# Cross attention of a fused attention and expert kernel rebuilt: heads on halves of TensorE, late normalisation, a ring of eight x tiles, and paced transfers

## The chip, the cores and the metric

The kernel runs on one core of a Trainium2 chip. The metric is the device time of one execution in microseconds (us), median of three runs. One core has five engines that are programmed apart and meet at semaphores: TensorE (PE; matmuls and transposes into PSUM, which has 8 banks of 128 x 512 floats), VectorE (DVE), ScalarE (ACT), GpSimd (POOL, which doesn't read PSUM here) and SyncE (SP, which only issues DMAs here). Each engine runs its own list of instructions strictly in order.

## The reference, cut to what matters

```python
def xattn(q, k, v, gamma):               # q: (4, 512, 512); k = v = ctx, same shape; 8 heads
    qh, kh, vh = (a.reshape(B, 8, 64, 512) for a in (q, k, v))
    qk = einsum('bhdq,bhdl->bhql', qh, kh) / sqrt(64)
    return gamma * einsum('bhql,bhdl->bhdq', softmax(qk, -1), vh).reshape(B, 512, 512)
x = x + xattn(layernorm(x), ctx_2048, ctx_2048, gamma)
h = layernorm(x).reshape(-1, 512)        # 2048 rows
# shared expert, 1408 wide, times a sigmoid gate; router: softmax over 8, top 2, weights normed
# routed experts, 352 wide: silu(h @ w_gate[e]) * (h @ w_up[e]) @ w_down[e], weighted by the router
x = x + routed + sigmoid(h @ shared_gate_w) * shared
```

Everything is float32. A matmul operand a is split into a rounded high part (type fp32r) and the rest, and a product is made of three terms, hi*hi, hi*lo and lo*hi, each an fp32r matmul. A row of 64 consecutive rows of x is one head's query, so a tile of 128 rows is two heads.

## The kernel before, in words

**Stages.** Attention over 16 tiles (NT) of 128 rows; then the shared expert in 4 blocks of 512 rows by 11 chunks of 128 hidden columns (`gate_up`, `down`, `weights_hi`, `weights_lo`); then 39 slots of 128 rows for the routed experts. All three are written out as one list for each engine.

**One attention tile.** SP loads x (`xb`), the context tile twice over (`cn` in rows, `cd` with each head's 64 rows doubled onto 128 partitions) and x a second time (`x2b`). DVE takes the row moments, POOL the inverse deviation and the shift (`rstd`, `nmr`), ACT writes the normed rows (`xn`, L657) and the high part of the queries (`qs`, L668), POOL their low part (L531). POOL splits the doubled keys (`kh`, `kl`). A head's `qs` has high and low part on the two halves of the partitions, against the doubled keys, so that two matmuls (L1233, L1234) give all terms of a score block of 128 x 512: 16 matmuls a tile. DVE takes the row maximum (L924), ACT the exponential with the row sum (L681), DVE the reciprocal, and POOL multiplies the probabilities by it (L548). Only then does PE transpose them (`probs_T`, L1241, 4 transposes for each of 8 groups), ACT and DVE split them (`pth` L687, `ptl` L933), and three matmuls for each group (L1254, L1255, L1257) sum the output of both heads in one bank. DVE adds gamma times that to `x2b` (L939). One tile later the new rows are normed (ACT, L661), transposed (`rows_T`), evicted (`x2T`, L693) and used for the router (`logits`), and stored three times: `x_rows`, `x_normed_rows`, `x_normed_transposed`.

**Order.** Every engine's list is written by hand in `tile(t, ...)`: tiles 0 to 3 and the last two are written out, the ten between run as a loop on each engine (`over_tiles`, `Fori`). PE works on head 0 and 1 of tile t while the scores of tile t + 1 are slipped in between.

**Start.** SP issues the loads of tiles 0 and 1, a few small ones, two zero tiles and then `slot_rows` (L378), a table of 4992 entries of 8 bytes, and behind it the loads of tile 2.

**End of attention.** PE ends tile 15, runs the first chunk of the shared expert (`gate_up(0, 0)`), then `rows_T(15)` and `logits(15)`, then the second chunk. SP stores the last `x2T` (L362) and only then issues the loads of weight chunk 2 (`load_chunk`, L389). ACT waits for the stores, then runs silu of chunk 0, `weights_hi(2)`, which waits for chunk 2, and `hidden_hi(0)`, on which `down(0, 0)` (L1361) waits through DVE.

## Time and profile before

| | |
|---|---|
| median of 3 runs (lowest, highest) | 927.79 us (927.32, 928.38) |
| the profiled execution: its own time | 931.45 us |
| its span, from first to last instruction | 929.1 us |
| mean granted TensorE clock | 0.985 of full speed |
| PE busy | 871.1 us, 94% of the span |
| attention, to the first matmul of the shared expert | 0 to 283.7 us |
| shared expert | 283.7 to about 646 us |
| routed experts | about 646 to 929 us |

The page of the profile gives busy times by engine and the chain of work that ended last. A matmul's record lasts until its result is complete (0.39 us for 512 columns), and the next starts before that, so the distance between starts is the price of one in a stream. A line of the timeline merges instructions that follow each other with the same shape and source line: start, time covered, engine, line, operation, what is written and read, count, and in brackets the idle time before it and what ended it.

### The profile page before, as it was taken

What the parts mean: (1) busy time and instruction counts of PE and PEld (TensorE: products, weight loads), DVE (VectorE), ACT (ScalarE), POOL (GpSimd) and SP (SyncE); (2) the same over time, 40 slices, a digit from 0 to 9 for tenths busy, and PEclk for the clock granted to TensorE, in tenths of its full rate; (3) what the DMA queues carried; (4) which work ended last, traced back from release to release, by engine and by line L of the source; (5) the groups of instructions that cost most, each with busy time, mean ns of one, the idle gap of its engine ahead of it and who ended that gap; (6) DMA issues with size and microseconds to landing.
All of it is one profiled execution on the core that took longest, in us unless ns stands there. A gap on an engine that the chain in (4) does not pass through costs nothing.

```text
span 929.1 us, 14497 instructions
## 1 busy us (share of the span) xinstructions
PE 871.1 (94%) x4560; PEld 746.0 (80%) x4560; DVE 571.9 (62%) x920; ACT 519.0 (56%) x879; POOL 477.9 (51%) x460
## 2 busy tenths in 40 slices
PE   4798998999998999999999999999999999999993
PEld 3587777877776888888888888888899999999992
DVE  5587878787874653442121212113899999999892
ACT  5588788887884432112111111112688888888881
POOL 5587787878740000004333000000589999999984
PEclk9899999999999999999999999999999999999997
DMA  9435334253553431400032002553954344443542
GB/s 135 86 101 158 116 123 149 97 162 103 161 190 127 134 102 46 136 0 1 1 137 25 0 1 91 187 187 104 335 104 86 74 83 75 79 80 68 91 62 40
DMA packets 70142, 93.77 MB, mean 101 GB/s; under 512 B 16137, under 2 KB 35593, under 8 KB 70098
## 3 DMA queue, kind: packets, MB, share of 16 engines
q1 hardware_dynamic: 60338, 72.73, 26.7%
q0 software_dynamic: 9760, 20.49, 12.4%
q8 instruction: 24, 0.39, 0.2%
q14 instruction: 20, 0.16, 0.1%
HBM read 65.59 MB, written 27.60 MB: 100 GB/s over the span
## 4 chain that ended last, share of the span: by engine, by line
PE 70%; ACT 2%; DVE 1%; issue 1%; DMA 0%; POOL 0%; POOLq 0%; SPq 0%; ACTq 0%; DVEq 0%
PE bank L1347 8%; PE bank L1349 8%; PE bank L1348 8%; PE bank L1414 5%; PE bank L1416 5%; PE bank L1415 5%; PE bank L1361 4%; PE bank L1363 4%; PE bank L1362 4%; PE bank L1439 3%; PE bank L1438 3%; PE bank L1440 3%; PE bank L1371 2%; PE bank L1425 1%; PE bank L1241 1%
## 5 line engine op out<-in xcount | busy, mean ns | idle before, releaser
L1035 DVE TENSOR_TENSOR sg<-bank,sg 128x512 f32<-128x512 f32 x44 | 30.4, 692 | 208.8 <-PE bank L1349 200.0
L1347 PE MATMUL bank<-x_hl,wsp 128*128 128x512 f32 x352 | 137.1, 390 | 0.0
L1349 PE MATMUL bank<-x_hl,wsp 128*128 128x512 f32 x352 | 137.0, 389 | 0.0
L1348 PE MATMUL bank<-x_hl,wsp 128*128 128x512 f32 x352 | 137.0, 389 | 0.0
L593 POOL DMA_INDIRECT slot_rows<-msrc,posi x32 | 36.1, 1128 | 176.2 <-PE bank L1349 169.8
L608 POOL DMA_INDIRECT xg<-x_normed_rows,meta x39 | 39.8, 1021 | 159.7 <-PE bank L1371 142.1
L787 ACT ACTIVATE sg<-bank 128x512 f32<-128x512 f32 x44 | 26.3, 598 | 158.4 <-PE bank L1349 158.4
L687 ACT ACTIVATE pth<-bank 128x512 fp32r<-128x512 f32 x128 | 73.4, 598 | 52.0 <-PE bank L1241 50.4
L933 DVE TENSOR_TENSOR ptl<-bank,pth 128x512 fp32r<-128x512 f32 x128 | 85.9, 682 | 21.1 <-ACT pth L687 20.9
L548 POOL TENSOR_SCALAR pb<-pb,rinv 128x512 f32<-128x512 f32 x128 | 87.7, 699 | 13.2 <-DVE rinv L929 7.8
L794 ACT ACTIVATE hh<-sg 128x512 fp32r<-128x512 f32 x44 | 27.8, 631 | 114.2 <-DVE sg L1035 99.5
L681 ACT ACTIVATE pb<-bank,negmax 128x512 f32<-128x512 f32 x128 | 86.9, 689 | 0.7 <-DVE negmax L924 0.3
L924 DVE TENSOR_REDUCE negmax<-bank 128x1 f32<-128x512 f32 x128 | 81.9, 681 | 0.7 <-PE bank L1234 0.2
L629 POOL TENSOR_TENSOR wd<-wex,wd 96x512 fp32r<-96x512 f32 x39 | 76.3, 1957 | 3.3
L1233 PE MATMUL bank<-kh,qs 128*128 128x512 f32 x128 | 57.9, 453 | 21.2 <-POOL qs L531 18.1
L1241 PE MATMUL bank<-ident,pb 128*128 128x128 f32 x512 | 72.9, 276 | 4.6 <-POOL pb L548 4.6
L619 POOL DMA_INDIRECT out<-y,meta x39 | 71.0, 1821 | 11.9 <-issue 5.7
L1349 PEld LDWEIGHTS bank<-x_hl,wsp 128*128 128x128 f32 x352 | 66.1, 188 | 13.7
L1348 PEld LDWEIGHTS bank<-x_hl,wsp 128*128 128x128 f32 x352 | 66.1, 188 | 13.7
L1347 PEld LDWEIGHTS bank<-x_hl,wsp 128*128 128x128 f32 x352 | 66.1, 188 | 13.7
L1241 PEld LDWEIGHTS bank<-ident,pb 128*128 128x128 f32 x512 | 62.3, 143 | 15.9 <-POOL pb L548 5.5
L1361 PE MATMUL bank<-wsp,hh 128*128 128x512 f32 x176 | 68.8, 391 | 2.3 <-DVE hl L1037 1.7
(157 smaller groups left out, 2354.2 us busy)
## 6 DMA issues: line engine op xcount, KB each, us to landing
cd<-in_ctx SPq DMA_DIRECT2D x32, 256.0 KB, 4.8
wex<-in_L_ffn_w_gate SPq DMA_DIRECT2D x8, 704.0 KB, 4.3
...
```

Source lines behind the costliest of these rows:

```text
L548: gp.tensor_scalar(pb[s][:, q, :], pb[s][:, q, :], rinv[:, s, q:q + 1], 0.0, ALU.mult, ALU.add).then_inc(g_pn, 1)
L619: g.indirect_dma_start(out=out, out_offset=bass.IndirectOffsetOnAxis(ap=meta[:, s, 0:1], axis=0), in_=y3[s % 2][:, :], in_offset=None, com ...
L629: gp.tensor_tensor(wd3[0:IR, 1, c], wex[0:IR, e, 2 * W3 + (IC - 1) * H:EW], wd3[0:IR, 0, c].bitcast(F32), ALU.subtract).then_inc(g_wd, 1)
L681: sc.activation(pb[s][:, q, :], bS[q][:, :], ACT.Exp, bias=negmax[:, s, q:q + 1], scale=1.0, accum_out=rsum[:, s, q:q + 1]).then_inc(a_exp, 1)
L687: sc.activation(pth[c][:, :], bT[c % 2][:, :], ACT.Copy).then_inc(a_pth, 1)
L924: ve.tensor_reduce(negmax[:, s, q:q + 1], bS[q][:, :], AX_X, ALU.max, negate=True).then_inc(d_max, 1)
L933: ve.tensor_tensor(ptl[c][:, :], bT[c % 2][:, :], pth[c][:, :].bitcast(F32), ALU.subtract).then_inc(d_ptl, 1)
L1241: ins = te.transpose(bT[c % 2][:, q * P:(q + 1) * P], pb[s][:, q, c * P:(c + 1) * P], ident[:, :])
L1347: te.matmul(bk[:, :], hi, xhi, start=(h == 0), stop=False)
L1348: te.matmul(bk[:, :], hi, xlo, start=False, stop=False)
L1349: ins = te.matmul(bk[:, :], lo, xhi, start=False, stop=(h == HC - 1))
L1361: te.matmul(bY[tt][:, :], th, hi, start=(c == 0), stop=False)
```

## The change

Nothing changes from the shared expert on, but for three points at the seam. In attention:

- **Scores.** Each head's queries and keys stay on their own 64 partitions (`qh`, `ql`, `kh`, `kl`, 128 x 512 each). For one block of 128 query columns, `scores(t, c)` runs three terms for both heads: six matmuls over 64 partitions, alternately partitions 0 to 63 into one PSUM bank and 64 to 127 into the next. 24 matmuls of 64 partitions a tile stand for 16 of 128. The context is loaded once, not three times.
- **Maxima** go over both heads at once (128 x 1024, four a tile in place of eight of 128 x 512).
- **Normalisation** moves behind the value product. PE transposes the unnormed probabilities as soon as the exponentials are done. POOL spreads the eight reciprocals over 64 columns each (`spread`), PE transposes that (`inverses`, 4 transposes more), ACT evicts it times gamma (`rgam`), and POOL multiplies the attention output by it (`scaled`) and adds x (`residual`).
- **Values.** A head's high and low values stand side by side as one 128-column weight, so two matmuls a group do in place of three; the two halves of the result are added by an ACT copy (`low_half`) and a DVE addition over 64 partitions (`halves`), for each head.
- **Engines.** The normed rows and the high parts of the queries move from ACT to POOL.
- **Ring and pace.** x is loaded once into a ring of 8 buffers, in which the new rows are made in place. SP lets each load off at a count of PE's transposes (`paced`).
- **Loop.** All engines' steps are written out (`over_tiles` from -4 to 18), but for PE, whose steps 4 to 13 are a loop over pairs.
- **Seam.** `gate_up(0, 0)` comes after step 16, then step 17 (`rows_T(14)`, `logits(14)`), `gate_up(0, 1)`, and step 18 (`rows_T(15)`, `logits(15)`). Block 0 and chunks 0 and 1 are loaded in step 12.

In a middle tile, on SP: the stores of the new rows and the loads of the context. Before (`xb`, `cd` and `cn` are loads; `x2b` both):

```order
L356 DMA x_rows<-x2b_96 128x512 [waits d_x2]
L358 DMA x_normed_rows<-x2n_98 128x512 [waits a_x2n]
L352 DMA x2b_96<-in_x 128x512 [waits st_x21,a_x2n]
L344 DMA cn_71<-in_ctx 128x512 [waits e_vt]
L335 DMA xb_70<-in_x 128x512 [waits a_xn]
L340 DMA cd_74<-in_ctx 64x2x512 [waits kl_done]
L340 DMA cd_74<-in_ctx 64x2x512
```

Now (`g_x2` counts `residual` on POOL):

```order
L352 DMA x_rows<-xb_84 128x512 [waits g_x2]
L356 DMA x_normed_rows<-x2n_109 128x512 [waits g_x2n]
L343 DMA cn_69<-in_ctx 128x512 [waits kl_done,e_vt,e_t]
L360 DMA x_normed_transposed<-x2T_111 128x512 [waits a_x2T]
L338 DMA xb_81<-in_x 128x512 [waits st_x20,g_x2n,e_t]
```

Before, the store waited for DVE's L939, and keys came in `cd`; now the load of `cn`, keys and values of step i + 2, stands behind the store of the rows of tile i - 1.

On POOL in the same place. Before:

```order
L538 TENSOR_SCALAR kh_75<-cd_73 128x1024 [waits ld_cd0,e_s]
L548 TENSOR_SCALAR pb_86<-pb_86,rinv 128x512 [waits d_rinv]
L548 TENSOR_SCALAR pb_86<-pb_86,rinv 128x512
L519 TENSOR_TENSOR rstd<-vare,mhalf 128x1 [waits d_vare1,a_x2n]
L521 TENSOR_SCALAR nmr<-aggr,rstd 128x1 [waits g_rstd1]
L531 TENSOR_TENSOR qs_82<-xn_80,qs_82 64x512 [waits a_qh,g_nmr1]
```

Now (`d_att` counts `halves`; L562 is `scaled`, L566 `residual`):

```order
L562 TENSOR_TENSOR att_104<-att_104,rgam 128x512 [waits a_Rg,d_att]
L516 TENSOR_SCALAR nmr<-aggr,rstd 128x1 [waits g_rstd1]
L566 TENSOR_TENSOR xb_85<-xb_85,att_104 128x512 [waits g_att]
L522 TENSOR_SCALAR xn<-xb_88,rstd,nmr 128x512 [waits g_nmr0]
L539 CAST kh_72<-cn_70 128x512 [waits e_s,ld_cn1]
L528 CAST qh_76<-xn 128x512 [waits e_s,g_xn]
L550 TENSOR_SCALAR x2n_109<-xb_84,rstd,nmr 128x512 [waits e_x2T,st_x2n1,g_nmr1]
L533 TENSOR_TENSOR ql_78<-xn,qh_76 128x512 [waits g_qh]
L543 TENSOR_TENSOR kl_74<-cn_70,kh_72 128x512 [waits g_kh]
```

The keys' high part used to be made a tile ahead of its use, between multiplications of probabilities; now the split of keys and queries follows `residual` directly, and `cn`'s landing is waited for inside it.

On PE at the seam. Before, behind the last matmul of `gate_up(0, 0)`:

```order
L1275 MATMUL bank<-ident,x2n_98 128x128 [waits a_lg,a_x2n]
L1275 MATMUL bank<-ident,x2n_98 128x128 x3
L1281 MATMUL bank<-rgT,x2T_100 128x9 [waits a_x2T]
L1281 MATMUL bank<-rgT,x2T_100 128x9 x3
L1347 MATMUL bank<-x_hl,wsp_104 128x512 [waits d_wl]
```

Now, behind the last matmul of `gate_up(0, 1)`:

```order
L1259 MATMUL bank<-ident,x2n_109 128x128 [waits g_x2n,a_x2T]
L1259 MATMUL bank<-ident,x2n_109 128x128 x3
L1265 MATMUL bank<-rgT,x2T_111 128x9 [waits a_x2T,a_lg]
L1265 MATMUL bank<-rgT,x2T_111 128x9 x3
L1362 MATMUL bank<-wsp_113,hh_130 128x512 [waits d_hl,g_x2,a_lg]
```

Tile 15's transposes moved behind 24 more matmuls, and `down(0, 0)` follows them directly. The diff, cut to its core:

```diff
         big = cursor[0]
...
-        vs = [place(f"vs{j}", [P, 2, LC, 3, DH], F32R) for j in range(2)]
-        pb = [place(f"pb{j}", [P, QC, L]) for j in range(2)]
+        kh = [place(f"kh{j}", [P, L], F32R) for j in range(2)]
+        kl = [place(f"kl{j}", [P, L], F32R) for j in range(2)]
+        qh = [place(f"qh{j}", [P, L], F32R) for j in range(2)]
...
+            def load_x(t):
+                after(sp, g_x2n, t - NX + 1)
+                after(sp, st_x2[t % 2], 16 * ((t - NX) // 2 + 1))
+                sp.dma_start(xb[t % NX][:, :], x_t[t, :, :]).then_inc(ld_x[t % NX], 16)
...
+            def load_values(t):
+                after(sp, e_vt, t - 1)
                 after(sp, kl_done, t - 1)
-                for half in range(2):
-                    sp.dma_start(cd[par][DH * half:DH * (half + 1), :, :], c_h[t, :, :, :]).then_inc(ld_cd[par], 16)
-            def load_values(t, par):
-                after(sp, e_vt, t - 1)
-                sp.dma_start(cn[par][:, :], c_t[t, :, :]).then_inc(ld_cn[par], 16)
...
+            def paced(t, n):
+                if there(t):
+                    sp.wait_ge(e_t, 8 * t + n)
+            def store_rows(t):
+                sp.wait_ge(g_x2, t + 1)
+                sp.dma_start(x2_t[t, :, :], xb[t % NX][:, :]).then_inc(st_x2[t % 2], 16)
...
+            def step(i):
+                if there(i - 1):
+                    store_rows(i - 1)
+                if there(i - 3):
+                    store_normed(i - 3)
+                if there(i + 2):
+                    paced(i - 1, 8)
+                    load_values(i + 2)
+                if there(i - 3):
+                    store_columns(i - 3)
+                if there(i + 4):
+                    paced(i, 3)
+                    load_x(i + 4)
...
+            load_x(0)
+            load_values(0)
+            load_x(1)
+            load_values(1)
+            load_x(2)
+            small_ones()
+            load_x(3)
+            for i in range(NT + 3):
+                step(i)
...
-            def power(kind, n):
-                after(g, (a_xn, a_x2n)[kind], n)
-                g.wait_ge(d_vare[kind], n + 1)
-                gp.tensor_tensor(rstd[:, kind, :], vare[:, kind, :], mhalf[:, :], ALU.pow).then_inc(g_rstd[kind], 1)
-                wait_ahead(g, g_rstd[kind], n + 1)
-                gp.tensor_scalar(nmr[:, kind, :], aggr[:, kind, 0:1], rstd[:, kind, :], -1.0, ALU.mult, ALU.mult).then_inc(g_nmr[kind], 1)
...
-            def queries_lo(t, s, par, before, count):
-                g.wait_ge(before, count)
-                g.wait_ge(a_qh, 2 * t + s + 1)
-                r = slice(DH * s, DH * (s + 1))
-                o = slice(DH * (1 - s), DH * (2 - s))
-                gp.tensor_tensor(qs[s][o, :], xn[par][r, :], qs[s][r, :].bitcast(F32), ALU.subtract).then_inc(ql_done, 1)
...
+            def queries(t):
+                g.wait_ge(g_nmr[0], t + 1)
+                gp.tensor_scalar(xn[:, :], xb[t % NX][:, :], rstd[:, 0, t % 2, :], nmr[:, 0, t % 2, :], ALU.mult, ALU.add).then_inc(g_xn, 1)
...
+                g.wait_ge(g_xn, t + 1)
+                after(g, e_s, 8 * t - 8)
+                gp.tensor_copy(qh[t % 2][:, :], xn[:, :]).then_inc(g_qh, 1)
...
-            def norm_p(k, s, pair):
-                wait_ahead(g, d_rinv, 2 * k + pair + 1)
-                for q in (2 * pair, 2 * pair + 1):
-                    gp.tensor_scalar(pb[s][:, q, :], pb[s][:, q, :], rinv[:, s, q:q + 1], 0.0,
-                                     ALU.mult, ALU.add).then_inc(g_pn, 1)
...
+            def step(i):
+                if there(i + 1):
+                    queries(i + 1)
+                    keys_hi(i + 1)
+                    queries_hi(i + 1)
+                if there(i - 3):
+                    rows_normed(i - 3)
+                if there(i + 1):
+                    queries_lo(i + 1)
+                    keys_lo(i + 1)
+                if there(i - 2):
+                    inverse_deviation(1, i - 2)
+                if there(i + 2):
+                    inverse_deviation(0, i + 2)
+                if there(i):
+                    spread(i)
+                if there(i + 2):
+                    shift(0, i + 2)
+                if there(i - 1):
+                    scaled(i - 1)
+                if there(i - 2):
+                    shift(1, i - 2)
+                if there(i - 1):
+                    residual(i - 1)
...
+            def inverses(t):
+                act.wait_ge(e_R, t + 1)
+                after(act, g_att, t)
+                sc.activation(rgam[:, :], bT[1][:, :], ACT.Copy, scale=gam[:, :]).then_inc(a_Rg, 1)
+            def low_half(t, s):
+                act.wait_ge(e_pv, 8 * t + 4 * s + 4)
+                after(act, d_att, 2 * t - 1 + s)
+                lo, hi = slice(DH * (1 - s), DH * (2 - s)), slice(DH * s, DH * (s + 1))
+                sc.activation(lob[hi, :], bO[lo, :], ACT.Copy).then_inc(a_lob, 1)
...
-            def maxima(k, s, pair):
-                after(dve, a_exp, 4 * k - 4)
-                for q in (2 * pair, 2 * pair + 1):
-                    dve.wait_ge(e_s, 4 * k + q + 1)
-                    ve.tensor_reduce(negmax[:, s, q:q + 1], bS[q][:, :], AX_X, ALU.max, negate=True).then_inc(d_max, 1)
...
+            def maxima(t, c):
+                dve.wait_ge(e_s, 8 * t + 2 * c + 2)
+                after(dve, a_exp, 8 * t + 2 * c - 6)
+                ve.tensor_reduce(negmax[:, c, :], bSS[c % 2][:, :, :], AX_X, ALU.max, negate=True).then_inc(d_max, 1)
...
+            def halves(t, s):
+                dve.wait_ge(a_lob, 2 * t + s + 1)
+                after(dve, g_x2, t - 1)
+                r = slice(DH * s, DH * (s + 1))
+                ve.tensor_tensor(att[t % 2][r, :], bO[r, :], lob[r, :], ALU.add).then_inc(d_att, 1)
...
+            def scores(t, par, c):
+                if c == 0:
+                    pe.wait_ge(ql_done, t + 1)
                     pe.wait_ge(kl_done, t + 1)
-                after(pe, a_exp, 4 * k - 4 + 2 * pair + 2)
-                for q in (2 * pair, 2 * pair + 1):
-                    te.matmul(bS[q][:, :], qs[s][:, q * P:(q + 1) * P], kh[par][:, s, :], start=True, stop=False)
-                    te.matmul(bS[q][:, :], qs[s][:, q * P:(q + 1) * P], kl[par][:, s, :], start=False, stop=True).then_inc(e_s, 1)
...
+                after(pe, a_exp, 8 * t + 2 * c - 2)
+                terms = ((qh, kh), (qh, kl), (ql, kh))
+                for n, (a, b) in enumerate(terms):
+                    for s in range(2):
+                        r = slice(DH * s, DH * (s + 1))
+                        ins = te.matmul(bSS[c % 2][:, s, :], a[par][r, c * P:(c + 1) * P], b[par][r, :], start=(n == 0), stop=(n == 2))
+                        if n == 2:
+                            ins.then_inc(e_s, 1)
...
-                    ins = te.transpose(bT[c % 2][:, q * P:(q + 1) * P], pb[s][:, q, c * P:(c + 1) * P], ident[:, :])
+                    ins = te.transpose(bT[P_BANK[n]][:, q * P:(q + 1) * P], pb[par][s][:, q, c * P:(c + 1) * P], ident[:, :])
...
-                hi, lo = (vs[par][:, a, c, s:s + 2, :].rearrange("p a d -> p (a d)") for a in range(2))
-                first, last = s == 0 and c == 0, s == 1 and c == LC - 1
-                pe.wait_ge(a_pth, 4 * k + c + 1)
-                te.matmul(bO[:, :], hi, pth[c][:, :], start=first, stop=False)
-                te.matmul(bO[:, :], lo, pth[c][:, :], start=False, stop=False)
-                pe.wait_ge(d_ptl, 4 * k + c + 1)
-                te.matmul(bO[:, :], hi, ptl[c][:, :], start=False, stop=last).then_inc(e_pv, 1)
+                if c == 0:
+                    after(pe, d_att, 2 * t + s)
+                v = vs[par][:, c, 2 * s:2 * s + 2, :].rearrange("p a d -> p (a d)")
+                pe.wait_ge(a_pth, 8 * t + n + 1)
+                te.matmul(bO[:, :], v, pth[n % 4][:, :], start=(c == 0), stop=False)
+                pe.wait_ge(d_ptl, 8 * t + n + 1)
+                te.matmul(bO[:, :], v, ptl[n % 4][:, :], start=False, stop=(c == LC - 1)).then_inc(e_pv, 1)
...
+                pe.wait_ge(g_rspr, t + 1)
+                for c in range(QC):
+                    ins = te.transpose(bT[1][:, c * P:(c + 1) * P], rspr[:, 2 * c:2 * c + 2, :].rearrange("p s d -> p (s d)"), ident[:, :])
+                ins.then_inc(e_R, 1)
...
-                    values_T(t + 1, i + par, 1 - par)
...
+                        gate_up(b, c, par)
                     if b == 0 and c == 1:
                         pe.wait_ge(a_lg, NT)
-                        pe.wait_ge(d_x2, NT)
+                        pe.wait_ge(g_x2, NT)
...
                 if last:
                     rows3(1, 0, 1)
-            logits(NT - 2, 0)
+            for i in range(-4, 4):
+                step(i, i // 2, i % 2)
+            with pe.Fori(2, NI - 1) as half:
+                for par in range(2):
+                    step(2 * half + par, half, par)
+            for i in range(NT - 2, NT + 1):
+                step(i, i // 2, i % 2)
             gate_up(0, 0, 0)
-            rows_T(NT - 1, 1)
-            logits(NT - 1, 1)
+            step(NT + 1, (NT + 1) // 2, (NT + 1) % 2)
+            gate_up(0, 1, 0)
+            for i in range(NT + 2, NT + 3):
+                step(i, i // 2, i % 2)
             for b in range(NB):
                 block2(b, b % 2, b == NB - 1)
```

## Rows read from the trace of the kernel before

**Rows 1.** The page: the span.
```profile
span 929.1 us, 14497 instructions
```
**Rows 2.** Windows: stretch, length, busy us (count) of each engine, clock, DMA share, GB/s.
```profile
180.00:220.00 40.00, 37.23 (x222) 31.27 (x221) 32.00 (x67) 32.92 (x76) 32.38 (x40) 1.00 0.41 125
```
**Rows 3.** Timeline: PE's value transposes (L1265) seven tiles apart, the next group behind one.
```profile
151.38 0.60 PE L1265 MATMUL bank<-ident,cn 128*128 128x128 f32 x4
...
151.81 0.60 PE L1241 MATMUL bank<-ident,pb 128*128 128x128 f32 x4
...
263.54 0.60 PE L1265 MATMUL bank<-ident,cn 128*128 128x128 f32 x4
```
**Rows 4.** Waits of PE from 30 to 260 us: us in total, times, longest.
```profile
PE bank L1233 <- POOL qs L531: 18.1, 18, 1.5
```
**Rows 5.** Groups by line, 100 to 220 us: count | busy us, mean ns | idle before.
```profile
L548 POOL TENSOR_SCALAR pb<-pb,rinv 128x512 f32<-128x512 f32 x60 | 41.1, 700 | 3.4 <-POOL qs L531 3.4
L681 ACT ACTIVATE pb<-bank,negmax 128x512 f32<-128x512 f32 x60 | 40.7, 689 | 0.2
L933 DVE TENSOR_TENSOR ptl<-bank,pth 128x512 fp32r<-128x512 f32 x60 | 40.2, 681 | 7.5 <-ACT pth L687 7.5
L924 DVE TENSOR_REDUCE negmax<-bank 128x1 f32<-128x512 f32 x59 | 37.8, 681 | 0.3
L687 ACT ACTIVATE pth<-bank 128x512 fp32r<-128x512 f32 x60 | 34.4, 598 | 20.4 <-PE bank L1241 19.5
...
L542 POOL TENSOR_TENSOR kl<-cd,kh 128x1024 fp32r<-128x1024 f32 x8 | 19.2, 2395 | 0.0
```
**Rows 6.** Timeline of the start: the one DVE instruction over 128 x 1024.
```profile
8.39 1.21 DVE L949 TENSOR_TENSOR kl<-cd,kh 128x1024 fp32r<-128x1024 f32 x1
```
**Rows 7.** Timeline of PE: matmuls of 9 partitions between matmuls of 128.
```profile
15.38 0.40 PE L1233 MATMUL bank<-kh,qs 128*128 128x512 f32 x1
15.62 0.39 PE L1234 MATMUL bank<-kl,qs 128*128 128x512 f32 x1
15.94 0.41 PE L1292 MATMUL bank<-ident,rg 9*128 9x9 f32 x4
16.28 0.50 PE L1233 MATMUL bank<-kh,qs 128*128 128x512 f32 x1
```
**Rows 8.** The start: timeline, the landing of `slot_rows`, windows around the stall.
```profile
8.23 0.49 SPq L378 DMA_DIRECT2D slot_rows<-meta  x1
...
20.19 1.09 PE L1241 MATMUL bank<-ident,pb 128*128 128x128 f32 x8 [2.71 <-POOL pb L548]
...
30.00 0.69 DVE L896 BATCH_NORM_STATS2 stats<-xb 128x6 f32<-128x512 f32 x1 [3.71 <-DMA xb<-in_x]
...
DMA to landing us min/median/max: 21.4/21.4/21.4
...
32.00:36.00 4.00, 2.17 (x9) 2.10 (x10) 1.16 (x3) 0.76 (x2) 3.74 (x6) 0.50 0.23 75
```
**Rows 9.** SP's issues in a middle tile, and `cn`'s landing, 100 to 240 us.
```profile
152.58 0.35 SPq L352 DMA_DIRECT2D x2b<-in_x  x1
153.03 0.40 SPq L344 DMA_DIRECT2D cn<-in_ctx  x1
...
DMA to landing us min/median/max: 2.7/2.9/3.3
```
**Rows 10.** Timeline of the end of attention.
```profile
268.31 1.03 PE L1241 MATMUL bank<-ident,pb 128*128 128x128 f32 x8
...
283.70 0.48 PE L1347 MATMUL bank<-x_hl,wsp 128*128 128x512 f32 x1
...
289.27 0.60 PE L1275 MATMUL bank<-ident,x2n 128*128 128x128 f32 x4
289.91 0.60 ACT L693 ACTIVATE x2T<-bank 128x512 f32<-128x512 f32 x1 [1.96 <-PE bank L1275]
...
298.86 0.47 PE L1361 MATMUL bank<-wsp,hh 128*128 128x512 f32 x1 [1.68 <-DVE hl L1037]
```

680 lines of the change are left out of this document (305 added, 375 removed).

## The prediction

> **What bounds the kernel now.** I read the windows first, then the groups by line, then the timelines of the start, a middle tile and the end of attention. Only attention changes. A middle tile lasts (263.54 - 151.38) / 7 = 16.02 us [rows 3]. In 40 us of it PE is busy 37.2, DVE 32.0, ACT 32.9, POOL 32.4 [rows 2], so per tile PE 14.9, DVE 12.8, ACT 13.2, POOL 13.0 us. PE bounds, and what it misses it waits mostly for POOL's low part of the queries, 18.1 us in 230 [rows 4]. Around that: the start, where PE's first transposes of probabilities stand at 20.19 and DVE waits for x until 30.00, behind a table of tiny packets that took 21.4 us from 8.23 [rows 8]; and the seam, where the first transposes of tile 15 stand at 268.31, the shared expert starts at 283.70 and its first `down` at 298.86 [rows 10]. I reckon to that `down`; what follows (929.1 - 298.9 = 630 us [rows 1, 10]) is unchanged.
>
> **The work per tile after.** PE: a group of four transposes costs 151.81 - 151.38 = 0.43 us [rows 3], a matmul of 512 columns 0.23 to 0.24 [rows 7]. One group more, +0.43; 8 value matmuls fewer, -1.84. The scores were 16 x 0.23 = 3.7. If the two heads' halves run side by side, 12 pairs cost 2.8 (-0.9); if they don't, 24 matmuls cost 5.5 (+1.8). The switch to smaller operands and back cost 0.32 and 0.34 us where a matmul follows after 0.24 [rows 7], so about 0.1 a switch and 8 x 0.1 = +0.8. PE: 14.9 + 0.43 - 1.84 - 0.9 + 0.8 = **13.4**, or **16.1** if the halves run in turn. No row has two matmuls on disjoint partitions, so the ends are 0.23 and 0.46 a pair. I take the low one: the two heads use other partitions and other PSUM banks, and the next weight is loaded beside a running matmul already.
> The Trainium skill (TensorEngine Tiling (Array Packing), Key Properties) says that tiles load and multiply in parallel, and that each change of the tiling mode drains the engine. The first would give 13.4 and the second speaks against the change; the 0.1 us of [rows 7] is all that this trace shows of such a drain.
> DVE: eight maxima of 0.68 [rows 5] become four of about 1.21, the one row over 1024 columns [rows 6]: -0.6; L939 goes, two `halves` come at 0.68: +0.6; six fewer tiny ones: -0.5. About **12.3**. ACT: four evictions and norms of queries and rows go (-2.9), three copies come at 0.60 (+1.8): **12.1**. POOL: eight multiplications of 0.70 go, the key split halves (L542 2.395 to 1.2 [rows 5]), five one-input passes at 0.70 and four two-input ones at 1.2 stay or come, plus 1.7 of tiny ones: **10**. On busy time alone a tile would be 13.4 plus the few tenths that PE loses to others, say 14.0. That the steps are written out, or loop on PE, I price at nothing: no row separates it, and PE would have 15.0 - 13.4 = 1.6 us a step to hide it (below); if that cover were gone I bound it at 0.3 us a step either way, 4 us in all.
>
> **The loop through the DMA.** The order makes a wait that busy time hides. SP's `store_rows(i-1)` waits for `residual(i-1)`, and the load of `cn` for tile i+2 is queued behind it. POOL needs that load for `keys_hi(i+2)`, nearly next in its list; behind it are queued the split of the queries, the normed rows of tile i-2 and `keys_lo`; PE's `scores(i+2, 0)` waits for these, and behind it stand the value products and the first transposes; DVE's maximum and, later, the next `halves`. From the end of `halves` of one step: `scaled` and `residual` 2 x 1.2 and 0.5 of handing over, 2.9; two store issues at 153.03 - 152.58 = 0.45 before the load [rows 9], 3.8; landing 2.9 [rows 9], 6.7; three passes at 0.70 and two at 1.2, 11.2; hand over, three pairs of scores, one value pair and a group of transposes with its end, 13.1; ACT's `pth` 0.60, 13.8; DVE's `ptl` 0.68, or PE's last value pair with ACT's `low_half`, 14.5; `halves` 0.68, 15.1 [rows 5]. So a step can't be shorter than about **15.0 us**, a us above what the engines need. With the landing at 2.7 or 3.3 [rows 9], and copies on POOL at 0.55 to 0.8 us, it is 14.5 to 15.5.
>
> **Start.** The first chain (moments, POOL's five passes, scores, maxima, exponentials) comes to the same 20.3 as before by my count: no wait for the norm on POOL, but four exponentials of each head must be done. The table now has 4 transfers of 256 KB fewer ahead of it and is issued some 2.5 us sooner; it should land near 26.5, not 29.6. x of tile 3 is behind it, and DVE's list has its moments first in step 1, from about 23: a wait of 3.4 us with all DVE work queued behind. Then a DVE step's work, 12.3 + 0.7: the first second-head `halves` ends at 39.4. Thirteen loops later: 39.4 + 13 x 15.0 = 234.4. Step 15 has no load to wait for; its first transposes stand some 9.9 us on, at **244.3** (before 268.3).
>
> **Seam.** From there to the shared expert before: 15.4 us [rows 10]. Now DVE has splits of tokens and two weight chunks in the same stretch, with one `halves` more: 15.9, at 260.2. Then `gate_up(0, 0)` 24 x 0.23 = 5.5; `rows_T(14)`, its eviction and `logits(14)` 2.2; `gate_up(0, 1)` 5.5; `rows_T(15)` to the end of its eviction 290.51 - 289.27 = 1.24 [rows 10]; from that end to `down(0, 0)` 298.86 - 290.51 = 8.35 [rows 10], a chain of store issue, load of chunk 2, `weights_hi(2)`, `hidden_hi(0)` and DVE that the change doesn't shorten. Sum 22.8: 283.0. Before, `gate_up(0, 1)` covered 5.5 of these 8.35 us; now nothing but `logits` is left, and PE stands for some 7.5 us. After the stall of the start the granted clock was 0.50, 1.2 in place of 2.4 GHz, for the 4 us of one window [rows 8]; 36 matmuls of 0.23 follow here, and half speed for 4 to 5 us costs +2.4: **285.4**. Before: 298.86.
>
> **Sum.** 298.9 - 285.4 = 13.4 us gained: span 915.7; the profiled execution would be 931.45 - 13.4 = 918.0, and the median, 3.7 below it before, **914.4 us**. Each 0.1 us a step is 1.3 us; the gain is gone at a step of 16.0.
>
> **Rivals.** (a) The loop doesn't bind, since the landing or POOL's passes are shorter, or the 7 us at the seam are covered: steps of 14.0, 914.4 - 13 = 901.4 us, or 904 by the seam alone. For it: POOL's 10 us of work. Against: the order leaves no way round. (b) More waits join the loop, since ACT and DVE must each be free just then and x2n's transposes wait for POOL too: a step of 15.9, 914.4 + 0.9 x 13 = 926 us. For it: three engines above 12 us and 15 us a step. (c) The two halves of the array run in turn. PE then has 16.1 us a tile, with 0.2 of waits 16.3: 914.4 + 1.3 x 13 = **931.3 us**, slower than before. It decides from 0.45 us a pair of score matmuls. Against: disjoint partitions and banks.
>
> **How the numbers follow.** Forecast 0.45, its own range 908 to 921; (a) 0.22, 893 to 908; (b) 0.20, 921 to 930; (c) 0.13, 926 to 938. Faster than by 0.2% (1.9 us, what this measurement can tell from no change) are the forecast, (a) and some 0.6 of (b): 0.79; within it 0.06; slower 0.15. Range 900 to 929.
>
> **What would show it.** Right: steps of about 15 us; POOL idle some 3 us a step before `kh` until DMA `cn` lands, 35 to 40 us in all; PE waiting for POOL `kl` at the first scores of a tile; `slot_rows` landing near 26; PE idle 7 us before the first `down`, clock 0.5 behind it. Score pairs 0.23 apart show the halves together, singles 0.23 apart show (c). No wait for `cn` with steps of 14 is (a). Wrong altogether: waits of ACT or DVE on instruction issue in the written-out steps.

## Result and the profile after

The changed kernel takes **930.5 us** (median of 20 runs, 926.3 to 935.3) beside 927.6 us for the kernel before on the same chips (20 runs, 921.7 to 933.0). The ratio is 1.0031 with an interval of 1.0016 to 1.0047: slower by 0.3%. The forecast was 914.4 us, with a range of 900 to 929. It was wrong by 16 us, and the sign was wrong.

The page of the changed kernel, its span and the busy time of each engine, beside [rows 1]:

```profile
span 927.5 us, 13748 instructions
## 1 busy us (share of the span) xinstructions
PE 859.2 (93%) x4624; PEld 713.7 (77%) x4624; DVE 573.2 (62%) x820; ACT 507.1 (55%) x863; POOL 433.5 (47%) x414
```

The span of the one profiled execution is 1.6 us *shorter* than before, while the medians say 2.9 us *longer*. So the two traces tell where time went, and the medians alone tell which kernel is faster. The profiled execution of before happened to lie 3.7 us above the median of its three runs; that of after lies 1.2 us below its own.

Windows of the changed kernel (stretch, length, busy us (count) of PE, PEld, DVE, ACT, POOL, granted clock, DMA share, GB/s): a stretch of attention, to be read against [rows 2], and the stretch of the seam.

```profile
180.00:220.00 40.00, 34.85 (x232) 25.40 (x230) 34.03 (x57) 32.26 (x77) 24.98 (x33) 1.00 0.39 128
...
260.00:300.00 40.00, 28.65 (x131) 23.35 (x132) 16.86 (x25) 16.50 (x25) 6.36 (x9) 0.83 0.43 139
```

PE had 37.2 of 40 us to do and now has 34.9, and no engine is full. The steps hardly shrank all the same. The value transposes (L1253) of tiles 2 and 15 stand at 37.54 and 242.51, so 13 steps take 15.77 us each, where [rows 3] gave 16.02 for seven middle ones and the same 13 took 16.16 before. Waits of the changed kernel from 40 to 250 us (engine, what it was to do, what it waited for: us in total, times, longest), beside [rows 4]:

```profile
POOL kh L539 <- DMA cn<-in_ctx: 43.5, 13, 4.4
...
PE bank L1259 <- POOL x2n L550: 15.5, 12, 2.3
POOL rspr L556 <- DVE rinv L922: 13.1, 13, 1.6
POOL att L562 <- DVE att L933: 12.6, 13, 1.2
```

POOL stands 3.3 us in each of 13 steps until `cn` has landed, and PE then waits for POOL. That is the loop which the prediction described. Its links in one middle step, from the timelines of DVE, POOL, SP and PE in turn (start, us, engine, line, operation; in brackets the idle time before it and its releaser):

```profile
144.17 0.69 DVE L933 TENSOR_TENSOR att<-bank,lob 64x512 f32<-64x512 f32 x1
...
159.63 0.69 DVE L933 TENSOR_TENSOR att<-bank,lob 64x512 f32<-64x512 f32 x1
```
```profile
144.95 1.28 POOL L562 TENSOR_TENSOR att<-att,rgam 128x512 f32<-128x512 f32 x1 [0.94 <-DVE att L933]
...
146.43 1.29 POOL L566 TENSOR_TENSOR xb<-xb,att 128x512 f32<-128x512 f32 x1
...
151.52 0.61 POOL L539 CAST kh<-cn 128x512 fp32r<-128x512 f32 x1 [3.04 <-DMA cn<-in_ctx]
...
154.65 1.28 POOL L543 TENSOR_TENSOR kl<-cn,kh 128x512 fp32r<-128x512 f32 x1
```
```profile
147.75 0.32 SPq L352 DMA_DIRECT2D x_rows<-xb  x1
148.11 0.43 SPq L356 DMA_DIRECT2D x_normed_rows<-x2n  x1
148.66 0.39 SPq L343 DMA_DIRECT2D cn<-in_ctx  x1
```
```profile
156.17 0.51 PE L1216 MATMUL scores<-kh,qh 64*128 64x512 f32 x2 [0.57 <-POOL kl L543]
...
157.64 0.60 PE L1225 MATMUL bank<-ident,pb 128*128 128x128 f32 x4
```

Read it as a ring. The second head's `halves` ends at 144.86; `scaled` and `residual` end at 147.72; SP had been held by the store of x_rows, issues it, then the store of the normed rows, then the load at 148.66; it lands 2.86 us later, at 151.52; the low part of the keys ends at 155.93; the scores follow, then transposes, ACT, DVE, and the next `halves` ends at 160.32. That is 2.86 + 0.94 + 2.86 + 4.41 + 4.39 = 15.46 us.

The seam, from the timeline of PE, beside [rows 10]: the first transposes of tile 15, the first `gate_up`, `rows_T(15)`, its `logits`, the first `down`, and the first matmul of the `gate_up` behind it.

```profile
252.10 0.63 PE L1225 MATMUL bank<-ident,pb 128*128 128x128 f32 x4 [0.21 <-DVE ptl L926]
...
270.54 0.48 PE L1348 MATMUL scores<-x_hl,wsp 128*128 128x512 f32 x1
...
283.94 0.60 PE L1259 MATMUL bank<-ident,x2n 128*128 128x128 f32 x4
285.31 1.03 PE L1265 MATMUL bank<-rgT,x2T 128*128 128x9 f32 x8 [0.78 <-ACT x2T L697]
294.03 0.77 PE L1362 MATMUL bank<-wsp,hh 128*128 128x512 f32 x1 [7.68 <-DVE hl L1010]
...
299.29 0.43 PE L1348 MATMUL scores<-x_hl,wsp 128*128 128x512 f32 x1
```

The shared expert starts 13.2 us sooner than before (270.54 for 283.70), but its first `down` only 4.8 us sooner (294.03 for 298.86): `gate_up(0, 1)` no longer stands over the chain from `rows_T(15)`. Twelve matmuls then take 5.26 us; before, they took 2.8 (298.86 to 301.71) at a granted clock of 1.00. Here the clock behind the 7.68 us of idle time is at the lower of its two levels, 1.2 GHz, as the window over them shows (columns as above):

```profile
294.00:299.00 5.00, 4.97 (x12) 3.94 (x13) 4.24 (x6) 3.15 (x5) 0.00 (x0) 0.50 0.41 107
```

So 2.4 us are left where the next `gate_up` starts (301.7 before, 299.29 now), and 0.8 go on the rest.

### The profile page after: what moved, and what is told of

It is laid out like the page before. It is cut to its first block, busy times and chain, and to the rows that moved or that the text cites. A ratio compares the mean times of both kernels' runs of the same rounds, so it can differ in the third digit from the quotient of the medians.

```text
span 927.5 us, 13748 instructions
## 1 busy us (share of the span) xinstructions
PE 859.2 (93%) x4624; PEld 713.7 (77%) x4624; DVE 573.2 (62%) x820; ACT 507.1 (55%) x863; POOL 433.5 (47%) x414
## 4 chain that ended last, share of the span: by engine, by line
PE 74%; POOL 11%; issue 8%; DVE 3%; ACT 2%; DMA 2%; POOLq 0%; SPq 0%; DVEq 0%; ACTq 0%
PE scores L1348 9%; PE scores L1349 9%; PE scores L1350 9%; PE bank L1362 4%; PE bank L1364 4%; PE bank L1363 4%; PE bank L1449 3%; PE bank L1448 3%; PE bank L1450 3%; PE scores L1216 3%; PE scores L1424 3%; PE scores L1426 3%; PE scores L1425 3%; PE bank L1424 3%; PE bank L1426 3%
## 5 line engine op out<-in xcount | busy, mean ns | idle before, releaser
L1008 DVE TENSOR_TENSOR sg<-scores,sg 128x512 f32<-128x512 f32 x44 | 30.4, 692 | 216.4 <-PE scores L1350 202.2
L1348 PE MATMUL scores<-x_hl,wsp 128*128 128x512 f32 x352 | 137.2, 390 | 0.0
L1350 PE MATMUL scores<-x_hl,wsp 128*128 128x512 f32 x352 | 137.0, 389 | 0.0
L1349 PE MATMUL scores<-x_hl,wsp 128*128 128x512 f32 x352 | 137.0, 389 | 0.0
L779 ACT ACTIVATE sg<-scores 128x512 f32<-128x512 f32 x44 | 26.3, 598 | 160.5 <-PE scores L1350 160.5
L926 DVE TENSOR_TENSOR ptl<-bank,pth 128x512 fp32r<-128x512 f32 x128 | 87.8, 686 | 23.7 <-ACT pth L678 23.2
L678 ACT ACTIVATE pth<-bank 128x512 fp32r<-128x512 f32 x128 | 76.7, 600 | 39.7 <-PE bank L1225 38.9
L672 ACT ACTIVATE pb<-scores,negmax 128x512 f32<-128x512 f32 x128 | 88.1, 695 | 12.7 <-DVE negmax L916 12.7
L916 DVE TENSOR_REDUCE negmax<-scores 128x2 f32<-128x1024 f32 x64 | 77.9, 1216 | 16.6 <-PE scores L1216 16.6
L1225 PE MATMUL bank<-ident,pb 128*128 128x128 f32 x512 | 80.6, 282 | 4.3 <-DVE ptl L926 2.6
L1348 PEld LDWEIGHTS scores<-x_hl,wsp 128*128 128x128 f32 x352 | 66.2, 188 | 13.8
L1349 PEld LDWEIGHTS scores<-x_hl,wsp 128*128 128x128 f32 x352 | 66.1, 188 | 13.7
L1350 PEld LDWEIGHTS scores<-x_hl,wsp 128*128 128x128 f32 x352 | 66.1, 188 | 13.7
L1124 DVE TENSOR_TENSOR wg<-wex,wg 128x1408 fp32r<-128x1408 f32 x39 | 63.5, 1628 | 12.2 <-ACT wg L805 12.2
L1364 PE MATMUL bank<-wsp,hl 128*128 128x512 f32 x176 | 69.5, 395 | 0.0
```

Of the source, the lines that this page charges most:

```text
L672: sc.activation(pb[t % 2][s][:, c, :], bSS[c % 2][:, s, :], ACT.Exp, bias=negmax[:, c, s:s + 1], scale=1.0, accum_out=rsum[:, c, s:s + 1]) ...
L678: sc.activation(pth[n % 4][:, :], bT[P_BANK[n]][:, :], ACT.Copy).then_inc(a_pth, 1)
L916: ve.tensor_reduce(negmax[:, c, :], bSS[c % 2][:, :, :], AX_X, ALU.max, negate=True).then_inc(d_max, 1)
L926: ve.tensor_tensor(ptl[n % 4][:, :], bT[P_BANK[n]][:, :], pth[n % 4][:, :].bitcast(F32), ALU.subtract).then_inc(d_ptl, 1)
L1225: ins = te.transpose(bT[P_BANK[n]][:, q * P:(q + 1) * P], pb[par][s][:, q, c * P:(c + 1) * P], ident[:, :])
L1348: te.matmul(bk[:, :], hi, xhi, start=(h == 0), stop=False)
```

## Experiments

Times are medians, ratios are to the kernel before, run beside them on the same chip (927.4 to 928.8 us). "Step" is the mean of 13 steps, from the value transposes of tile 2 to those of tile 15 in the trace; "gate_up" and "down" are the starts of the first of each.

| kernel | us | ratio (interval) | step | gate_up | down |
|---|---|---|---|---|---|
| before | 927.6 | | 16.16 | 283.7 | 298.9 |
| changed | 930.5 | 1.003 (1.002-1.005) | 15.77 | 270.5 | 294.0 |
| e1_cn_first | 904.3 | 0.971 (0.966-0.977) | 13.60 | 244.4 | 269.4 |
| e2_rows_T_first | 923.0 | 0.994 (0.991-0.997) | 15.62 | 268.0 | 288.4 |
| e3_heads_in_turn | 926.2 (one run) | | 15.70 | 268.6 | |
| e5_both | 895.5 | 0.965 (0.962-0.969) | 13.60 | 239.7 | 258.6 |
| e6_written_out | 901.4 | 0.971 (0.967-0.975) | 13.60 | 243.6 | 268.9 |
| e7_one_store_less | 920.4 | 0.992 (0.989-0.994) | 15.34 | 266.1 | |
| e8_not_paced | 901.4 | 0.972 (0.968-0.975) | 13.60 | 241.6 | 266.4 |
| e9_chunk1_later | 894.6 | 0.964 (0.961-0.967) | 13.60 | 241.5 | 261.1 |
| e10_seam_ordered | 892.4 | 0.961 (0.958-0.964) | 13.60 | 244.3 | 258.2 |
| e11_all | 889.7 | 0.958 (0.956-0.961) | 13.60 | 243.2 | 258.8 |
| e12_one_store_more | 938.0 | 1.011 (1.008-1.015) | 16.53 | | |
| e13_tokens_later | 892.7 | 0.962 (0.959-0.965) | 13.60 | 241.1 | 261.3 |
| e14_all_tokens_later | 889.6 | 0.958 (0.955-0.961) | 13.60 | 242.2 | 256.3 |

**The loop, opened.** One edit in SP's `step`:

```diff
+                if there(i + 2):
+                    paced(i - 1, 8)
+                    load_values(i + 2)
                 if there(i - 1):
                     store_rows(i - 1)
                 if there(i - 3):
                     store_normed(i - 3)
-                if there(i + 2):
-                    paced(i - 1, 8)
-                    load_values(i + 2)
```

> SP's step issues the load of cn(i+2) ahead of the two row stores; nothing else changes. Theory L (the loop through store_rows, the load and POOL's keys sets the step; in the changed kernel 2.9 + 0.9 + 2.9 + 8.8 = 15.5 us from one second-head halves to the next): POOL's wait for cn goes from 43.5 us to under 2, and the step falls to what the fullest engine needs, 13.7 us for PE and some tenths of waits, 14.0 to 14.4 in place of 15.7; 11 to 13 such steps give 18 to 20 us: about 911 us. Rival W (the waits of the three engines on one another set the step as well, and another wait takes the place of this one): steps of 15.2 or more, 924 us or more.

904.3 us: 26 us faster than the changed kernel, 24 faster than before, and more than theory L had, since a step takes 13.60 us and not 14.0 to 14.4. In its trace the first line below is `kh` without a wait in the timeline of POOL, the second the window of 40 us that above showed PE at 34.85:

```profile
149.98 0.61 POOL L539 CAST kh<-cn 128x512 fp32r<-128x512 f32 x1
```
```profile
180.00:220.00 40.00, 40.00 (x272) 30.12 (x273) 37.49 (x62) 37.38 (x90) 25.93 (x34) 1.00 0.41 140
```

PE is now full, at 13.60 us a step, 2.2 us less than with the loop. Rival W falls: DVE and ACT at 37 of 40 us don't hold PE up. The whole change of the changed kernel was thus worth 24 us, and the place of one load took it away.

**The loop, by doses.** The load ahead of one of the two stores only, or behind a third. e7:

```diff
                 if there(i - 1):
                     store_rows(i - 1)
+                if there(i + 2):
+                    paced(i - 1, 8)
+                    load_values(i + 2)
                 if there(i - 3):
                     store_normed(i - 3)
-                if there(i + 2):
-                    paced(i - 1, 8)
-                    load_values(i + 2)
```

and e12:

```diff
-                if there(i + 2):
-                    paced(i - 1, 8)
-                    load_values(i + 2)
                 if there(i - 3):
                     store_columns(i - 3)
+                if there(i + 2):
+                    paced(i - 1, 8)
+                    load_values(i + 2)
```

> A dose of the loop: the changed kernel with the load of cn moved ahead of one of the two stores alone (x_normed_rows), still behind the store of x_rows that waits for residual. Theory L: each step is shorter by the one issue, 0.45 us, and the load has 256 KB less ahead of it, which took some tenths of its 2.9 us: steps of 15.0 to 15.2 in place of 15.7, 6 to 9 us over 13 steps, 921.5 to 924.5 us, POOL still waiting some 3 us for cn in each step. If only the loop's existence mattered and not its length (some other wait sets 15.7), no change: 930.

> The dose the other way: the changed kernel with the load of cn behind a third store (x2T's) in SP's list. One store less gave steps of 15.2 and 920.4 us. Theory L: 0.45 us more of issue and 256 KB more ahead of the load: steps of 16.0 to 16.3, 5 to 9 us more over 13 steps than 930.5, 936 to 940 us, slower than the kernel before by 1%. If the loop had slack there, 930.

The usual steps are as theory L had them, and so is e12's 938.0 us; e7's 920.4 lies 1.1 us below the range. Beside undisturbed steps of 15.6 in the changed kernel, those of e7 take 15.2 (115.23 to 130.39) and those of e12 16.0 (151.45 to 167.45). POOL's `kh` in two successive steps of e7, then a late one of e12:

```profile
135.87 0.61 POOL L539 CAST kh<-cn 128x512 fp32r<-128x512 f32 x1 [2.78 <-DMA cn<-in_ctx]
151.23 0.61 POOL L539 CAST kh<-cn 128x512 fp32r<-128x512 f32 x1 [2.95 <-DMA cn<-in_ctx]
```
```profile
174.79 0.61 POOL L539 CAST kh<-cn 128x512 fp32r<-128x512 f32 x1 [4.68 <-DMA cn<-in_ctx]
```

A store of 0.4 us in SP's list is 0.4 us a step: the loop has no slack in either direction. Thirteen such steps are worth 5 to 6 us. The medians differ by 10.1 and 7.5 us; what e7 has beyond that is not explained, since its traced execution, 927.8 us, was the slowest of its nine.

In a closed loop a late landing isn't absorbed either. In the changed kernel the time from the issue of `cn` to `kh` was mostly 3.0 to 3.1 us, but 4.2 (164.12 to 168.35) and 4.1 (227.78 to 231.89) in two steps, and these took 16.85 and 17.60. The second cost more than its delay: PE had idled for 2.25 us, the granted clock fell, and from the low part of the keys to the next `halves` it took 5.3 us in place of 4.4. Behind the first, PE had idled for 2.27 us and the clock stayed at 1.00, so whether such a wait costs clock isn't told by its length. The window over the second:

```profile
235.00:240.00 5.00, 5.00 (x23) 3.42 (x22) 2.09 (x4) 2.90 (x7) 1.96 (x4) 0.71 0.02 3
```

That e12's mean of 16.53 lies above its usual 16.0 is five such steps of 16.9 to 19.1 us, with 5.3 to 6.4 us in the same link, where 1.2 GHz stands in the windows (0.66 from 110 to 115 us, 0.50 from 178 to 182): part of the price of a longer loop is clock.

**The seam.** In the list of PE, `step(NT + 2)`, which is `rows_T(15)` and `logits(15)`, goes ahead of `gate_up(0, 1, 0)`; first in the changed kernel, then together with the open loop.

```diff
             step(NT + 1, (NT + 1) // 2, (NT + 1) % 2)
-            gate_up(0, 1, 0)
             for i in range(NT + 2, NT + 3):
                 step(i, i // 2, i % 2)
+            gate_up(0, 1, 0)
```

> PE's rows_T(15) and logits(15) are moved from behind gate_up(0, 1) to ahead of it; nothing else changes. Theory S (the chain from x2n(15) over its transposes, their store, the load of chunk 2 and weights_hi(2) to the first down runs uncovered): rows_T(15) moves from 283.9 to 278.4, the chain with it, and gate_up(0, 1) covers 5.5 us of it; the first down at 288.5 in place of 294.0, PE idle about 2.5 us before it in place of 7.7, and if the clock then stays at 1.00, 2.5 us more: 922.5 to 925 us. Rival: the chain is held elsewhere (the loads of chunk 2 queue behind other transfers, or ACT is busy), first down at 292 or later, 928 us or more.

> Both edits together: the load of cn ahead of the row stores (alone 904.3 us) and rows_T(15), logits(15) ahead of gate_up(0, 1) (alone 923.0 us, in place of 930.5 for the changed kernel). Theory L+S (they lie in different stretches, steps and seam, and add up): 904.3 - 7 = 897 us, steps of 13.6, first down near 261 to 264 at the full clock. Rival (the seam's gain was partly a shorter landing in the attention of that run): 904.3 - 4 = 900 us.

923.0 us (7.5 less) and 895.5 (8.8 less than with the loop alone); theory S holds for the chain, and the two add up as far as such medians tell. From the first `gate_up` to the end of the first `down` there were 28.8 us in the changed kernel; with e2 23.2 (267.99 to 291.2), 5.6 less. PE didn't idle before the `down`, but twice for 0.78 us in the exchange of evictions ahead of `gate_up(0, 1)`, and the clock, which S wanted at 1.00, fell all the same. That e2's first `down` stood at 288.4, where S put it, was partly luck: `gate_up(0, 1)` took 7.9 us in place of 5.5, and the shared expert had started 2.6 us sooner. In e5 that `gate_up` takes 8.2 us in place of 5.5; the first window below holds the exchange, the second `gate_up(0, 1)`:

```profile
245.00:250.00 5.00, 3.44 (x25) 2.89 (x24) 0.00 (x0) 1.37 (x3) 1.08 (x3) 0.93 0.71 270
250.00:255.00 5.00, 5.00 (x14) 4.03 (x15) 0.69 (x1) 3.10 (x4) 0.00 (x0) 0.50 1.00 299
```

That led to two more versions. e10 lays the transposes and logits of tiles 14 and 15 between the gate half and the up half of `gate_up(0, 1)`, and takes `silu(0, 0)` and the load of chunk 2 ahead of what they needn't wait for (the edits of ACT and SP aren't shown):

```diff
-            step(NT + 1, (NT + 1) // 2, (NT + 1) % 2)
-            for i in range(NT + 2, NT + 3):
-                step(i, i // 2, i % 2)
-            gate_up(0, 1, 0)
+            pe.wait_ge(a_x2T, NT - 2)
+            rows_T(NT - 2, 0)
+            gate_up(0, 1, 0, (0,))
+            pe.wait_ge(a_lg, NT - 2)
+            logits(NT - 2, 0)
+            pe.wait_ge(a_x2T, NT - 1)
+            rows_T(NT - 1, 1)
+            gate_up(0, 1, 0, (1,))
+            pe.wait_ge(a_lg, NT - 1)
+            logits(NT - 1, 1)
```

> From the kernel with both edits (895.5 us, first down at 258.6): rows_T and logits of tiles 14 and 15 are placed between the two halves of gate_up(0, 1), so that each eviction has 2.75 us of matmuls over it; ACT's silu(0, 0) and hidden_hi(0, 0) are ahead of the wait for all stores, and the load of chunk 2 ahead of the last row stores. The bubble there was 2.7 us of idle PE and 2.7 us of half clock (a span of 8.2 us for 24 matmuls that take 5.5). Expected: first down at 253.3, 5.3 us sooner, 890 us. Rival: weights_hi(2), which still waits for the last store, now holds gate_up(0, 2), and gives 2 to 5 us back: 892 to 895.

892.4 us. From `gate_up` to `down` 14.0 us in place of e5's 18.9, 4.9 of the 5.3 expected; PE waits 0.27 us there. Behind the `down` 0.8 us are lost again, 0.49 of them a wait for DVE's part of chunk 2 (`wsp`), which is the rival's way but not its 2 to 5 us. The median fell by 3.1 us, with intervals that overlap e5's. The attention of that trace started late by another cause (below), so its `gate_up` stands at 244.3.

e9 moves the conversion of weight chunk 1 on ACT and DVE behind the last probabilities of tile 15; e11 is e9 and e10 together.

> From the kernel with both edits (895.5 us): ACT's and DVE's conversion of weight chunk 1 (1.48 and 1.76 us) is moved behind the last probabilities of tile 15, since gate_up(0, 0) doesn't read it. In that kernel PE waits there 1.3 to 2.3 us at a time for DVE's ptl. If DVE's and ACT's lists set the stretch from T(15, 0) to the shared expert (17.7 us), it is 1.7 to 2.5 us shorter: 893 to 894 us. If PE's own waits for other things set it, no change.

> Both edits, chunk 1 later and the seam ordered. If the gains are of different places they add up: 895.5 - 5.3 - 2 = 888 us. If the one only moves waiting into the other, 890 to 893.

e9 missed: 894.6 us, not told apart from 895.5, and the way from the last value transposes to the shared expert is 27.0 us where it was 27.35. PE's wait of 2.34 us there is for `ptl(2)`, which stands in DVE's list ahead of chunk 1 and behind the split of the tokens; moving what comes after it can't help. e11 took 889.7, for 888 if both gains had added up; beside e10's 892.4 the intervals overlap.

**What the split of the tokens costs.** The prediction had 15.9 us from T(15, 0) to the shared expert; it took 18.4 (252.10 to 270.54). The timelines of DVE and of POOL there, in the changed kernel:

```profile
256.67 3.38 DVE L947 TENSOR_TENSOR x_hl<-x_hl 128x2048 fp32r<-128x2048 f32 x1 [0.89 <-ACT x_hl L710]
```
```profile
256.61 1.29 POOL L566 TENSOR_TENSOR xb<-xb,att 128x512 f32<-128x512 f32 x1
257.88 2.81 POOL L550 TENSOR_SCALAR x2n<-xb,rstd,nmr 128x512 f32<-128x512 f32 x1
```

L947 takes 2.28 us in its other three executions, and L550 0.77. The numbers close within 0.13 us if each waits for the other to end: POOL's residual ends at 257.90, 2.15 us more is 260.05, the end of L947; L550 ends 0.64 later. e13 moves L947 behind `ptl(2)` and `ptl(3)` in the kernel of e5, e14 in that of e11.

```diff
-                if i == NT:
-                    tokens_lo(0, 0)
                 if there(i):
                     maxima(i, 1)
                 ...
                 if there(i - 1):
                     probs_lo(i - 1, 3)
                 if i == NT:
+                    tokens_lo(0, 0)
                     weights_lo(0)
```

> From the kernel with both edits (895.5 us; there 17.7 us from T(15, 0) to the shared expert, the change's prediction had 15.9): DVE's split of the tokens (L947) goes behind ptl(2) and ptl(3) of tile 15. Theory P (POOL and DVE lock each other out: there L947 took 3.37 us in place of 2.28 behind POOL's residual, and POOL's x2n 2.81 in place of 0.77 behind L947): it starts when POOL has done both and takes 2.28 us, x2n 0.77, and PE no longer waits 2.3 us for ptl(2): the stretch is 1.1 to 1.5 us shorter, 893.5 to 894.5 us. If the 3.37 us is the price of a first use and not of POOL, it is 3.37 again and only the order counts: 0 to 0.5 us.

> All edits of the fastest version (889.7 us) and this one. Its stretch had the same pair of long instructions. Theory P: 1 to 1.5 us less, 888.5 us. Else 889.7.

The operations of e13, by tile (duration in ns min/median/max, first and last start, form), of DVE and of POOL:

```profile
L947 DVE TENSOR_TENSOR x_hl<-x_hl x4: 2281/2282/2284, 230.6 to 477.1; 128x2048 fp32r<-128x2048 f32 x4
```
```profile
L550 POOL TENSOR_SCALAR x2n<-xb,rstd,nmr x16: 765/776/785, 54.9 to 247.4; 128x512 f32<-128x512 f32 x16
```

Both long executions are gone: it was no price of a first use. The stretch gained less than the 1.1 to 1.5 us expected: it is 0.7 us shorter than in e5 (26.6 from the last value transposes, for 27.35) and 1.2 shorter in e14 than in e11 (26.8 for 27.95). The medians, 892.7 for 895.5 and 889.6 for 889.7, are too near to show it. The Trainium skill (SBUF — State Buffer, SBUF: two separate sides) says that the port pair which DVE and GpSimd share is locked for a whole instruction, also by a DVE operation with two inputs in SBUF, and that the other engine blocks. These traces agree with it within 0.13 us; and `ptl`, which reads one input from PSUM, stays at 0.68 us beside the same POOL work.

**The disputed costs of the change itself.** Three runs price what the prediction took on trust. e3 swaps the loops over heads and terms in `scores`:

```diff
-                for n, (a, b) in enumerate(terms):
-                    for s in range(2):
+                for s in range(2):
+                    for n, (a, b) in enumerate(terms):
```

> The six score matmuls of a chunk are issued head by head (three of the first, then three of the second) in place of in pairs, so that neighbours stand on the same 64 partitions. If pairs run side by side in the changed kernel (six matmuls in 0.89 us there), this takes 6 x 0.23 = 1.4 us a chunk and PE 2.0 us more a tile, 15.7 us of work against a loop of 15.7: steps of 16.3 to 16.8, 8 to 14 us longer than the changed kernel, 939 to 945 us. If the order of issue made no difference (each matmul takes its own time anyway), steps and time stay at 15.7 and 930.

The timeline of PE in the changed kernel, one chunk and the operation behind it:

```profile
159.87 0.50 PE L1216 MATMUL scores<-kh,qh 64*128 64x512 f32 x2
160.20 0.40 PE L1216 MATMUL scores<-kl,qh 64*128 64x512 f32 x2
160.44 0.39 PE L1216 MATMUL scores<-kh,ql 64*128 64x512 f32 x2
160.76 0.65 PE L1225 MATMUL bank<-ident,pb 128*128 128x128 f32 x4
```

And in e3:

```profile
154.75 0.51 PE L1216 MATMUL scores<-kh,qh 64*128 64x512 f32 x2 [0.57 <-POOL kl L543]
155.08 0.41 PE L1216 MATMUL scores<-kl,qh 64*128 64x512 f32 x2
155.32 0.40 PE L1216 MATMUL scores<-kh,ql 64*128 64x512 f32 x2
155.66 0.51 PE L1239 MATMUL bank<-pth,vs 128*128 128x512 f32 x1
```

Six matmuls of 512 columns in 0.89 us, for 6 x 0.23 = 1.4 in turn: the heads do run side by side, and rival (c) falls. My expectation of e3 fell too. Issued head by head they take 0.91 us, and the starts still stand in the same three pairs: the second head's three run beside the first's, though they stand three places further down the list. So these matmuls don't start in the order of PE's list, and what is said above of every engine, that it runs its list strictly in order, doesn't hold here. Its time, 926.2 us, is one run; steps of 15.70 for 15.77 say that nothing changed.

e6 writes out TensorE's steps 4 to 13 in place of the loop, e8 drops the waits of `paced`, both in the kernel of e1, where PE is full:

```diff
-            with pe.Fori(2, NI - 1) as half:
-                for par in range(2):
-                    step(2 * half + par, half, par)
+            for i in range(4, NT - 2):
+                step(i, i // 2, i % 2)
```

> The kernel with the load of cn first, with TensorE's steps 4 to 13 written out in place of the loop on the engine. PE is busy for the whole of a step there (13.6 us), so whatever the loop costs or saves shows. The prediction priced it at nothing: 904 us within 1.5, steps of 13.6. If written-out steps wait on instruction issue, steps are 0.1 to 0.3 us longer, 905.5 to 908 us; if the loop's jumps cost that, as much shorter, 900 to 903.

> The kernel with the load of cn first, without the waits that let the loads of cn and x off at set points of PE's work: they go as soon as their buffers are free. If pacing does nothing where the loop is open: 904 us within 1.5, steps of 13.6. If transfers started together slow each other or the queue fills and holds up the stores, steps of 13.7 or more and 906 or more; if pacing held something back, 900 to 902.

901.4 us each, steps of 13.60 us in both. The lowest of e1's four runs was 896.4 and the highest 904.4, so 3 us between medians tells nothing; the steps, equal to 0.01 us, do. Neither the loop on the engine nor the pacing costs or brings anything that the steps show.

**Where two executions of one kernel differ.** e4 is the kernel before once more.

> The kernel before once more, for a second trace: its profiled execution (931.45 us) lay 3.7 us above the median of its runs, and the trace of the changed kernel 1.2 below. If the span before the first down varies (DMA landings in attention), it is at 295 to 297 here in place of 298.9 where the time is 927 to 928; if the part behind varies, first down again at 298.9 and the rest 3 to 4 us shorter than 630.2.

929.9 us, span 927.5, first `down` at 297.28 in place of 298.86. The difference is at the start: DVE's wait for x of tile 3 behind the table of tiny packets ([rows 8], 3.71 us) is shorter here.

```profile
27.11 0.69 DVE L896 BATCH_NORM_STATS2 stats<-xb 128x6 f32<-128x512 f32 x1 [1.37 <-DMA xb<-in_x]
```

The changed kernel has the same lottery. In its trace the moments of tile 3 don't wait at all; in that of e10 they wait 2.9 us, a row of its waits from 14 to 45 us:

```profile
DVE stats L897 <- DMA xb<-in_x: 2.9, 1, 2.9
```

## The prediction, point by point

**Work per tile: right.** PE 13.4 us was forecast; with the loop open a step is all PE and takes 13.60. The parts hold too: a pair of score matmuls 0.24 us, the change to 64 rows and back 0.1 us each (0.33 in place of 0.24 at both ends of a chunk). DVE's maxima are 1.22 us as in [rows 6].

**The loop: the mechanism right, its length 0.75 us a step too short.** Link by link the forecast had 2.9 + 0.9 + 2.9 + 4.5 + 3.9 = 15.1, of which I took 15.0; one step measured 2.86 + 0.94 + 2.86 + 4.41 + 4.39 = 15.46. The link that was mis-sized is the last, from the low keys to the next `halves`: 2.35 us to ACT's `pth` behind the first transposes, not 1.9; what follows took 2.04 for 2.0. Of the 0.75 us this is 0.36, and 0.1 went when I took 15.0 for 15.1. The mean of 13 from `halves` to `halves` (36.75 to 241.57) is 15.75, and the rest is landings, for whose spread the sum had no term: they were mostly 3.0 to 3.1 us, two were over 4, and behind one of these the clock cost 0.9 us more. The two steps concerned, of 16.8 and 17.6, lie 3.5 us above two of 15.46. Against my count the loop is +9.8 us. Predicted waits of `kh` for the DMA were 35 to 40 us; 43.5 were found.

**Start: too late by 2.65.** `slot_rows` was to land near 26.5 and DVE to wait 3.4 us for x of tile 3. It landed 16.0 us after its issue at 5.21, at 21.2, and nothing waited; the first second-head `halves` ended at 36.75, not 39.4. By e10 and e4 this wait comes and goes between executions.

**T(15, 0) to the shared expert: 2.5 us short** (and 0.6 ahead of it). The 15.4 us of before, from which I started, had DVE's split of the tokens at 2.29 us with POOL idle beside it. Here POOL was at work, and the lock takes 1.1 us; with it gone, e13 gave 0.7 us. The other part is the order of DVE's list, by which PE waits 2.3 us for `ptl(2)`; how much each part of that order costs is not shown, since e9 and e13 moved only two pieces.

**Seam: right.** 22.8 + 2.4 us were forecast, 23.5 and 2.5 measured, with PE idle 7.68 before the `down` and the clock at 1.2 GHz behind it. What was left there was worth more than the change as it stood: e2 took back 7.5 us.

**The anchor: the second largest error.** These terms make -2.65 + 9.8 + 0.6 + 2.5 + 0.7 + 0.1, with 0.8 behind the `down` 11.9 us, which is the span's 927.5 - 915.7. The other 4.3 of the 16.1 us are no mechanism: I carried the 3.7 us by which the profiled execution of before lay above the median over to the median after. That of after lay 1.2 *below* its own; time and span are 1.8 apart there in place of 2.4. Single executions lay up to 0.6% from their median in these kernels, and the forecast gain was 1.4%.

**Rivals.** (a) said that the loop doesn't bind, 901 to 904 us: wrong for this kernel, and what one edit made of it, 904.3. (b), steps of 15.9 by more waits in the loop and 926 us, came nearest: 15.75. Its reason, three engines each free only now and then, is shown by e1 to be none, since they held no step up once the loop was open. (c) fell. No rival put late landings into a closed loop. The loop alone doesn't explain the sign: with steps of 15.75 the forecast would have been 914.4 + 9.8 = 924.2 us, still faster than before and inside the range. The stretch behind T(15, 0), 0.6 + 2.5 us, and the anchor, 4.3 us, made it slower, against the 2.65 us that the start gave. The prediction's chance of 0.15 for slower was nearly all on (c).
